# Layer 0 attention: block diagonals of keys and values by masked VectorE operations, values flat through DRAM

## What is computed

```python
x = x + jnp.tanh(g_xattn[0]) * _L0_xattn_ref(_layernorm(x, axis=-1), ctx_768, ...)
...
q = (query @ Wq + bq).reshape(B, Nq, H, D).transpose(0, 2, 1, 3)      # H = 16 heads, D = 16
k = (key_value @ Wk + bk).reshape(B, Nkv, H, D).transpose(0, 2, 1, 3)  # Nkv = 77
v = (key_value @ Wv + bv).reshape(B, Nkv, H, D).transpose(0, 2, 1, 3)
attn = jnp.einsum('bhqd,bhkd->bhqk', q, k) * scale
attn = jnp.clip(attn, -CLAMP, CLAMP)
attn = jax.nn.softmax(attn, axis=-1)
x = jnp.einsum('bhqk,bhkd->bqhd', attn, v).reshape(B, Nq, Cq)
return x @ Wo + bo
```

## Time and profile before

| | us |
|---|---|
| median of 3 runs (lowest, highest) | 1292.45 (1291.59, 1292.96) |
| the profiled execution, its time | 1293.61 |
| its span | 1291.8 |
| PE busy | 1161.7 (90%) |
| DVE busy | 917.2 (71%) |
| ACT busy | 849.7 (66%) |
| POOL busy | 530.3 (41%) |

### The profile page before, as it was taken

One profiled execution on the slowest core, in us unless ns is written; L12 is line 12 of the kernel. 1 busy time (PEld: TensorE's weight loads), 2 busy tenths in 40 slices (PEclk: granted clock), 3 DMA queues, 4 the chain that ended last, 5 costly groups with the idle time before them and its releaser, 6 DMA issues. The chain is left out here.

```text
span 1291.8 us, 25317 instructions
## 1 busy us (share of the span) xinstructions
PE 1161.7 (90%) x8357; PEld 875.0 (68%) x8357; DVE 917.2 (71%) x2043; ACT 849.7 (66%) x2409; POOL 530.3 (41%) x501
## 2 busy tenths in 40 slices
PE   5599999996895699999999999967999999959798
PEld 3578888884543477777777777744777777735476
DVE  3478787874752466666666668736999999769798
ACT  2477777772664456666666665526888888739897
POOL 3467677763223322222222222116888888600000
PEclk9799999998997799999999999988999999979899
DMA  3133333323885344333333342214424252200133
GB/s 104 49 104 98 108 95 95 102 82 121 276 209 159 110 82 142 117 115 115 117 117 117 117 119 87 74 57 137 145 71 146 69 151 69 63 9 1 33 103 127
DMA packets 131548, 135.98 MB, mean 105 GB/s; under 512 B 21225, under 2 KB 116127, under 8 KB 131295
## 3 DMA queue, kind: packets, MB, share of 16 engines
q1 hardware_dynamic: 123693, 115.19, 29.2%
q0 software_dynamic: 6816, 18.62, 5.5%
q10 hardware_dynamic: 914, 0.59, 0.2%
HBM read 84.43 MB, written 49.29 MB: 104 GB/s over the span
## 5 line engine op out<-in xcount | busy, mean ns | idle before, releaser
L1408 ACT ACTIVATE exp_h<-exp_ps_h,exp_b_now 128x256 f32<-128x256 f32 x312 | 129.1, 464 | 158.8 <-PE exp_ps_h L1348 155.0
L1322 POOL DMA_INDIRECT exp_xg<-xn,all_token_of x78 | 93.2, 1195 | 314.3 <-PE exp_ps_x L1335 293.3
L1348 PE MATMUL exp_ps_h<-exp_xhi,exp_w_now 128*128 128x256 bf16 x1248 | 214.6, 276 | 4.7 <-DVE exp_xlo L1439 4.7
L1793 ACT ACTIVATE a_z<-a_ps_sc,a_nmx 128x77 f32<-128x77 f32 x512 | 159.3, 366 | 33.6 <-DVE a_nmx L1895 33.6
L1348 PE MATMUL exp_ps_h<-exp_xlo,exp_w_now 128*128 128x256 bf16 x624 | 171.9, 276 | 0.0
L1515 DVE TENSOR_TENSOR exp_hlo<-exp_h,exp_hhi 128x512 bf16<-128x512 f32 x156 | 106.9, 692 | 81.2 <-ACT exp_hhi L1412 77.7
L1360 PE MATMUL exp_ps_y<-moe_w2s,exp_hhi 128*128 x624 | 147.4, 379 | 0.0
L1348 PEld LDWEIGHTS exp_ps_h<-exp_xhi,exp_w_now 128*128 128x128 bf16 x1248 | 123.4, 99 | 20.8 <-issue 5.3
L1793 ACT ACTIVATION_READ_ACCUMULATOR a_z<-a_ps_sc,a_nmx 128x1 f32 x512 | 126.9, 248 | 0.0
L1760 PE MATMUL a_ps_o<-a_v_now,a_phi 128*128 128x256 bf16 (+1 forms) x640 | 106.6, 273 | 2.3 <-DVE a_plo L1884 2.3
L434 PE MATMUL a_ps_vo<-a_pT,a_vblk 128*128 128x128 f32 (+1 forms) x704 | 88.5, 283 | 20.1 <-ACT a_pT L493 20.1
(11 more groups left out here) (241 smaller groups left out, 2772.0 us busy)
## 6 DMA issues: line engine op xcount, KB each, us to landing
a_stage<-in_L_ffn_W_dram SPq DMA_DIRECT2D x64, 256.0 KB, 3.2
y_slots<-exp_y SPq DMA_DIRECT2D x78, 128.0 KB, 1.7
fold_k<-route_kst SPq DMA_DIRECT2D x16, 308.0 KB, 4.3
fold_v<-route_vst SPq DMA_DIRECT2D x16, 308.0 KB
exp_job_in<-fold_k SPq DMA_DIRECT2D x14, 352.0 KB, 3.2
exp_job_in<-fold_v SPq DMA_DIRECT2D x14, 352.0 KB, 3.3
a_x<-in_x_dram SPq DMA_DIRECT2D x32, 128.0 KB, 2.8
x<-a_xo SPq DMA_DIRECT2D x32, 128.0 KB, 1.7
```

The costliest lines, as they stand in the source:

```text
L1322: pool.indirect_dma_start(out=xg[:, v, u, :], out_offset=None, in_=xn_dram[:, :], in_offset=bass.IndirectOffsetOnAxis(ap=at.bitcast(U32), ...
L1348: mm = pe.matmul(ps_h[:, i, f % 2 * SLOT_T:(f % 2 + 1) * SLOT_T], w1_now[:, v, k, hl, f * P:(f + 1) * P], xx[:, k, :], start=(q == 0), sto ...
L1408: ins = act.activation(h[:, f, :], ps_h[:, i, f % 2 * SLOT_T:(f % 2 + 1) * SLOT_T], ACT.Gelu_apprx_tanh, bias=b1_now[:, v, f:f + 1])
L1793: ins = act.activation(z[:, u, h * KEYS:(h + 1) * KEYS], ps_sc[:, j, (h - SB[j][0]) * KEYS:(h - SB[j][0] + 1) * KEYS], ACT.Exp, bias=nmx[: ...
```

## The change

place_keys, its kT of batch 0 and the four memsets go. POOL makes two masks instead, kmask (128 x 8) and vmask (128 x 11 x 8), by memset and affine_select. DVE writes kblk of a batch in one multiplication of the keys, broadcast over eight heads, with kmask (block_keys; for batch 0 straight from PSUM, before slot 0; for batch b+1 in slot 3 of batch b). For the values SP writes v_rows head by head to a DRAM tensor v_heads (1232 x 16 a batch) and reads it back with the 1232 rows along the partitions (v_flat, in the weights' buffer too), two batches at a time: place_values(0) in slot 1, place_values(1) in slot 4. DVE writes vblk in two multiplications with vmask (block_values; batch 0 in slot 2, batch b+1 in slot 5 of batch b). In slot 0 PE projects the values of the first two batches before the scores, ScalarE copies them right behind its qT.

```diff
+        v_flat = split["w1s"][:, E * KD - 2, :, :].rearrange("p c f -> p (c f)").bitcast(F32)[:, 0:B * RCH * dh].rearrange(
+            "p (b c d) -> p b c d", b=B, c=RCH)
...
-            def place_keys(b):
...
-            def place_values(b, h0, h1):
...
+            def place_values(pair):
+
+                bs = slice(2 * pair, 2 * pair + 2)
+                whole = (RCH - 1) * P
+                sp.wait_ge(s["v_rows_done"], pair + 1)
+                for b in (2 * pair, 2 * pair + 1):
+                    sp.dma_start(v_dram[b].rearrange("(h k) d -> k h d", h=HEADS),
+                                 v_rows[:, b, :].rearrange("k (h d) -> k h d", h=HEADS)).then_inc(v_out[pair], 16)
+                sp.wait_ge(v_out[pair], 32)
+                for b in (2 * pair, 2 * pair + 1):
+                    sp.dma_start(v_flat[:, b, 0:RCH - 1, :], v_dram[b, 0:whole, :].rearrange("(c p) d -> p c d", p=P)
+                                 ).then_inc(v_in[pair], 16)
+                    sp.dma_start(v_flat[0:ROWS - whole, b, RCH - 1, :], v_dram[b, whole:ROWS, :]).then_inc(v_in[pair], 16)
...
                 if T == 1:
-                    sp.wait_ge(s["zero_done"], 4)
-                    place_values(0, 0, HEADS)
-                if t == 6 and b + 1 < B:
-                    place_keys(b + 1)
-                if 2 <= t < 6 and b + 1 < B:
-                    place_values(b + 1, 4 * (t - 2), 4 * (t - 2) + 4)
+                    place_values(0)
+                if T == 4:
+                    place_values(1)
...
+                if T == 0:
+                    pe.wait_ge(weights_in, 16 * N_WEIGHTS)
+                    values(0, 2)
...
+            def block_keys(b):
+
+                wait(dve, s["scores_done"], NSB * TPB * (b - 1))
+                if b:
+                    dve.wait_ge(s["kT_done"], 1)
+                    rows = kT[:, :, b, :]
+                else:
+                    dve.wait_ge(s["mask_step"], 5)
+                    dve.wait_ge(s["k_proj"], 1)
+                    rows = ps_p[:, 0, 0:ng * KEYS].rearrange("p (g k) -> p g k", g=ng)
+                dve.tensor_tensor(kblk[:, b % 2, :, :].rearrange("p g (h k) -> p g h k", k=KEYS),
+                                  rows.unsqueeze(2).broadcast_to((P, ng, hpg, KEYS)),
+                                  kmask[:, :].unsqueeze(1).unsqueeze(3).broadcast_to((P, ng, hpg, KEYS)),
+                                  ALU.mult).then_inc(s["k_done"], 1)
+
+            def block_values(b):
+
+                dve.wait_ge(v_in[b // 2], 64)
+                wait(dve, s["pv_done"], TPB * (b - 1))
+                if b == 0:
+                    dve.wait_ge(s["mask_step"], 9)
+                for g, mine in vgroups:
+                    i0, n, c0 = mine[0], len(mine), blocks[mine[0]][0]
+                    ins = dve.tensor_tensor(vblk[:, b % 2, i0:i0 + n, :].rearrange("p i (h d) -> p i h d", d=dh),
+                                            v_flat[:, b, c0:c0 + n, :].unsqueeze(2).broadcast_to((P, n, hpg, dh)),
+                                            vmask[:, i0:i0 + n, :].unsqueeze(3).broadcast_to((P, n, hpg, dh)), ALU.mult)
+                ins.then_inc(s["v_done"], 1)
...
+                if T == 2:
+                    block_values(0)
+                if t == 3 and b + 1 < B:
+                    block_keys(b + 1)
+                if t == 5 and b + 1 < B:
+                    block_values(b + 1)
```

More of the change, by code:

```diff
@@ L149, in _, with attention @@
             act.wait_ge(tanh_done, 1)
-def attention(nc, C, x_in, x_out, w, gate_col, split):
+def attention(nc, C, x_in, x_out, w, gate_col, split, v_dram):
     hpg = 8
@@ L165, in attention @@
     pieces = pieces_of(hpg)
[L166 to L170, removed]
+    vgroups = [(g, [i for i, (c, gg) in enumerate(blocks) if gg == g]) for g in range(ng)]
     RING, SKEW, NZ = 8, 3, 3
@@ L181, in attention @@
         v_rows = split["w1s"][0:KEYS, E * KD - 1, :, :].rearrange("p c f -> p (c f)").bitcast(F32).rearrange("p (b d) -> p b d", b=B)
+        v_flat = split["w1s"][:, E * KD - 2, :, :].rearrange("p c f -> p (c f)").bitcast(F32)[:, 0:B * RCH * dh].rearrange(
+            "p (b c d) -> p b c d", b=B, c=RCH)
+        kmask = m.sb("kmask", [P, hpg])
+        vmask = m.sb("vmask", [P, len(blocks), hpg])
         kblk = m.sb("kblk", [P, 2, ng, hpg * KEYS])
@@ L208, in attention @@
         queries_in = m.sem("queries_in")
-        k_in = [m.sem(f"k_in{i}") for i in range(2)]
-        v_in = [m.sem(f"v_in{i}") for i in range(2)]
+        v_out = [m.sem(f"v_out{i}") for i in range(B // 2)]
+        v_in = [m.sem(f"v_in{i}") for i in range(B // 2)]
         x_loaded = [m.sem(f"x_loaded{i}") for i in range(RING)]
@@ L437, in slot @@
                 if T == 0:
-                    pe.wait_ge(weights_in, 16 * N_WEIGHTS)
-                    values(0, 2)
                     values(1, 1)
@@ L458, in _, with v_copy @@
             act.dma_start(gbo[:, :], w["bo"].partition_broadcast(P)).then_inc(weights_in, 16)
-            act.wait_ge(s["k_proj"], 1)
-            act.activation(kT[:, :, 0, :], ps_p[:, 0, 0:ng * KEYS].rearrange("p (g k) -> p g k", g=ng),
-                           ACT.Copy).then_inc(s["kT_done"], 1)
+            def v_copy(pair):
+                act.wait_ge(s["v_proj"], pair + 1)
+                act.activation(v_rows[:, 2 * pair:2 * pair + 2, :].rearrange("p b d -> p (b d)"),
+                               ps_p[0:KEYS, 2 - pair, :], ACT.Copy).then_inc(s["v_rows_done"], 1)
             turned(0)
@@ L506, in slot @@
                 if T == 0:
-                    for pair in range(B // 2):
-                        act.wait_ge(s["v_proj"], pair + 1)
-                        act.activation(v_rows[:, 2 * pair:2 * pair + 2, :].rearrange("p b d -> p (b d)"),
-                                       ps_p[0:KEYS, 2 - pair, :], ACT.Copy).then_inc(s["v_rows_done"], 1)
+                    v_copy(1)
                 if T == 1:
@@ L2279, in program @@
                   "wv": io["L0_xattn_Wv"], "bv": io["L0_xattn_bv"], "wo": io["L0_xattn_Wo"], "bo": io["L0_xattn_bo"]}
-            attention(nc, C, x_dram, x1_dram, w0, 0, split)
+            attention(nc, C, x_dram, x1_dram, w0, 0, split, v_dram)
             w1 = {"wq": io["L1_xattn_w_q"], "wkv": io["L1_xattn_w_kv"], "wo": io["L1_xattn_w_out"]}
```

38 lines of the change are left out of this document (27 added, 11 removed).

## The result

The change takes 1272.88 us (median of 4 runs, 1272.45 to 1273.40), the kernel before in the same series 1292.47: a ratio of 0.985, with a 95% interval of 0.984 to 0.987. The forecast was 1270.9. The profiled execution of the change took 1273.4 us around a span of 1271.3.

What follows compares the result with a forecast made beforehand. TensorE was taken to bound a steady slot at 7.92 us, with SP's issues delaying weight pieces. Start 18.8 + steady slots 6.5 - slot 5's 3.7 = 21.6 off 1293.61 gave 1272.0, median 1270.9 us; range 1267 to 1286.

Steps and rivals of the forecast that it cites:

- Start, scores of tile 1: Layer 0 attention: without waiting for key transfers, scores of tile 1 start near 27.05 instead of 30.18 us, gain 3.1.
- Slot 2: Weight piece no longer waits behind 25 value transfers, so the 23.64 us stretch becomes 7.92: gain 15.7 us.
- Steady slots: Later slots lose all late weight pieces, gain 6.5 us; VectorE's block operations of 1.42 and 1.77 us cost nothing.
- signs of being wrong: SP waiting over 8 us for a write, DVE standing at block_values(0), or slots 3, 11, 19, 5, 13, 21 over 8 us.
- rival B: VectorE binds in six slots with block operations: 1271.7 to 1280.5 us, chance 0.12.
- W: Time from first issue to last landing of a value round's two DRAM writes: 6.2 us, ends 4.2 and 27.2.
- my lower end: Shortest estimate for the DRAM writes: 13 ns an element, taken from the old 64 B pieces, giving 4.2 us.
- rule on the number of engines: Transfers use the largest engine count up to 16 dividing the slowest dimension: 11 for the writes, 1.4 us less gain.
- Slot 5: place_values(1) blocks SP in slot 4, so the next slot's weight piece is late: loss 3.7 us, clock holds.
- C: DRAM write slow but bearable, 7.8 to 13 us; slots 5 and 2 later, clock falls: 1274.3 to 1285.2, chance 0.2.
- D: Slower: small writes land as slowly as fold_scales by count, 27.2 us, both weight pieces late: 1316.6 us, chance 0.12.
- E: Start held by something hidden, late weights or POOL's masks; only 6.5 - 3.7 is left: 1289.6 us, chance 0.06.

Runs made afterwards that it cites:

- split kernel: The change with the second round's value reads moved to slot 5, behind its weight pieces, writes staying in slot 4: 1267.06 us, in another series 1268.68.

## Why the prediction was right, and where not

The direction, the place and nearly the size were right: 21.6 us forecast for the profiled execution, 20.2 measured. That the size is so near is in part luck: the start gave 1.44 us more than forecast, slots 2 to 4 took back 1.09 and slot 5 1.67.

- **Start, scores of tile 1: 3.1 forecast, 4.57 measured.** I let the first half of the values run at half pace to 20.6 us. They began at 16.64 and took 3.34, the scores at 19.81 already ran at full pace (2.24 us), and it was 5.80 us on to tile 1 in place of 6.45. The mechanism was the one named, PE without a gap; the experiment with the projection put back fits it.
- **Slot 2: 15.7 forecast, 15.25 measured.** The piece came in time and the clock held. The 0.47 missing is the length of slot 2 (8.39). VectorE is busy 8.25 of it, with block_values(0) in it at 2.37; that this paces the slot was not shown by a run.
- **Steady slots: 6.5 forecast, 6.54 measured.** All gone, with the block operations of slots 11, 13, 19 and 21 at no cost, as forecast. Slots 3 and 4 take 8.17 and 8.29, 0.62 us that the sum had at nothing, and slot 3 above 8 was one of the signs of being wrong; 0.37 of it comes with the key operation. The reason for no cost is also thinner than I had it: they take 2.12 and 2.37 us, not 1.42 and 1.77. I had the row that warned of it (a_xn, 2.81 us beside POOL's memsets, though that operation is of another form) and put it into rival B alone.
- **W: 6.2 forecast, 3.94 and 5.32 measured.** My 20 ns an element was too much: by the DMA share it is 12.5, and the 13 of my lower end was the price. So the elements took 1.9 us in place of 3.1, and issue and tail together 2.0 in place of 3.1; the lower end, 4.2, lay above the first value. The second round took 1.4 more: the store of a_xo and a load of x were issued 0.9 and 0.5 us ahead of it, and the engines were busy 0.56 of 5.32 us, 2.98, in place of 1.93. That covers 1.05 of the 1.38; the rest is open.

  The Trainium skill's rule on the number of engines, by which I had 7.6 (DMA: Bandwidth & Descriptors; it stands in the section "Why a DMA increments its semaphore by 16 and not by 1"), is not tested by that: no run shows how many engines took part.
- **Slot 5: 3.7 forecast, 5.37 measured; this is the step that failed.** The wait came at 3.77, but by two errors that cancel: with the W of 5.32, my W - 2.5 gives only 2.8, and most of the other microsecond is SP being there 0.4 late, the weight piece taking 4.1 from issue to use in place of 3.7, and ScalarE asking 0.3 earlier. What was wrong is "its clock fell only at the end of 5.4 us without work, so here it holds". It fell after 3.7 us of idle, and cost 1.6 us in pv; in the kernel with the old values it fell after 2.6. One sighting of a fall after 5.4 us gave an upper bound, and I used it as a threshold. The price of 3.0 us for a fall was too high for this one. The split kernel confirms the whole: 5.1 to 5.4 us less without the wait.

**The rivals.** B did not come true (slots 11, 13, 19 and 21 take 7.92 us) but for the 0.37 of slot 4, and doubled operations bring it about. The lower end of C should read 1275.4 (1292.45 less 17), not 1274.3; nothing hangs on it. C and D, the slow write, are refuted by W of 3.94 and 5.32, and from the other side by the run with 32-byte elements: at half the size and twice the number the writes took 6.7 and 7.5 us, where the 4-byte elements of fold_scales, 1024 of them, took 11.3. So the wait of fold_scales says nothing about elements of 32 and 64 bytes. E did not happen.

The Trainium skill's 512 bytes (DMA: Bandwidth & Descriptors, "Specifications"), by which I had 1316.6, do not show as such a time here: the 64-byte writes cost 12.5 ns of engine time each.

## What to carry to other kernels

A queue that feeds two customers is priced by what stands behind an item in it as well as by the item: 25 small transfers held back one weight piece and cost this kernel 12 us. Both customers were late, though: pv needs the values themselves, and with the piece alone in time at least 4.9 of the 10.15 us without work would have stayed. The cheap rival, the old transfers with the weight piece ahead of them, was not tried. When such a chain is replaced by "write, wait, read", put the wait behind the urgent issues of the slot; that one move gave 5 of the 25 us that the split kernel gains. And undo parts on a base without another wait behind them, and look at the stage as well as at the time, or a gain of 3 us reads as 0.7 or as a loss.

## What was not expected of the hardware

TensorE's clock fell to 1.2 GHz behind 3.5 to 3.9 us without work in four profiles. In three of them pv behind it took 4.26 to 4.32 us, in the kernel with the projection put back 5.03; after 5.7, 10.2 and 12.7 us of idle it took 5.03 to 5.04. The shortest idle time with a fall behind it is 2.61 us, in the kernel with the old values (pv in 4.32, the granted clock 0.50 from 76 to 78 us); after 1.70 and 1.87 us pv took 2.69. At the start of the kernel with the projection put back the column of the granted clock reads 1.00 from 14 to 22 us while scores take 4.47 us in place of 2.24: there it is the matmuls' own times, not the column, that show the half pace.

A DRAM write in elements of 64 or 32 bytes took 12.5 and 13.3 ns of engine time an element: halving the element did not halve its price.

VectorE's operation with two inputs in SBUF and the POOL operations of these rows, which read SBUF, exclude each other whole: VectorE's 1.42 us became 2.12, POOL's 0.55 became 1.74, and its 0.94 became 2.84.
